# Gated cross-attention and FFN block on one core: VectorE's steps for the next tile set between the splits of the third stage, and the splits of the second stage's last tile set ahead of the gammas and the base

## What is computed

```
x = x + tanh(g_xattn) * xattn(layernorm(x), ctx)
x = x + tanh(g_ffn)  * ffn(layernorm(x))

xattn(x): z = self_attn(x)            # causal, Q,K,V = x@Wq1, x@Wk1, x@Wv1
          x = layer_norm(x + z) * ln1_g + ln1_b
          z = cross_attn(x, ctx)      # 77 keys
          x = layer_norm(x + z) * ln2_g + ln2_b
          z = relu(x @ fc1_w + fc1_b) @ fc2_w + fc2_b
          return layer_norm(x + z) * ln3_g + ln3_b

ffn(x):   h = layernorm(x) * ln_gamma + ln_beta
          y = silu(h @ w1 + fc1_bias)     # w1: 512 x 2048, from codes and scales
          return x + 0.5 * (y @ w2 + fc2_bias)   # w2: 2048 x 512
```

## Time and profile before

| | us |
|---|---|
| median of 3 runs | 1725.01 |
| lowest and highest | 1722.39, 1727.16 |
| the profiled execution | 1726.05 |
| its span in the trace | 1724.2 |
| TensorE busy | 1658.7 |
| VectorE busy | 836.8 |
| ScalarE busy | 570.2 |
| GpSimd busy | 362.4 |

### The profile page before, as it was taken

The page is one execution under the profiler, slowest core; times in us unless marked ns, Lnnn a source line. Parts: engine busy times, 40 slices in busy tenths (PEclk is TensorE's granted clock), DMA queues, the critical chain, the costliest instruction groups (busy, mean ns, idle before and its releaser), DMA issues.

```text
span 1724.2 us, 20645 instructions
## 1 busy us (share of the span) xinstructions
PE 1658.7 (96%) x7734; PEld 1351.6 (78%) x7734; DVE 836.8 (49%) x1720; ACT 570.2 (33%) x990; POOL 362.4 (21%) x562
## 2 busy tenths in 40 slices
PE   6999999999999998899999799999999999999999
PEld 4877888877788887678777587878787878878787
DVE  4666554477664444578888854323322232232311
ACT  4442212135222211467566433222322232232222
POOL 0121110022110101278888711000000000000000
PEclk8999999999999999699999899999999999999999
DMA  6211111131121102635545232101010101010000
GB/s 203 73 50 67 63 37 37 38 110 59 64 74 37 43 19 95 222 123 166 159 161 176 100 122 73 50 1 49 0 49 1 49 0 49 1 43 7 17 9 25
DMA packets 68824, 117.24 MB, mean 68 GB/s; under 512 B 11201, under 2 KB 13249, under 8 KB 68571
## 3 DMA queue, kind: packets, MB, share of 16 engines
q1 hardware_dynamic: 64968, 110.12, 19.6%
q10 hardware_dynamic: 3757, 5.80, 1.1%
HBM read 81.05 MB, written 34.84 MB: 67 GB/s over the span
## 4 chain that ended last, share of the span: by engine, by line
PE 86%; DVE 6%; ACT 2%; POOL 2%; DMA 2%; issue 1%; ACTq 0%; SPq 0%; DVEq 0%
PE banks L652 80%; PE banks L662 3%; PE banks L785 2%; DVE split_q L1521 1%; ACT split_q L1017 1%; DVE plain L2029 1%; DVE split L1994 1%; DVE plain L2072 1%; DVE split L1521 1%; DMA plain<-in_L_xattn_Wq 1%; DMA plain<-in_L_xattn_fc_w 1%; DMA plain<-in_x 0%; ACT split L1017 0%; POOL split L1414 0%; POOL plain L1426 0%
## 5 line engine op out<-in xcount | busy, mean ns | idle before, releaser
L652 PE MATMUL banks<-split_q,split 128*128 128x512 f32 x2328 | 572.7, 395 | 5.4 <-POOL split L1414 5.1
L652 PE MATMUL banks<-split 128*128 128x512 f32 (+4 forms) x2292 | 550.1, 390 | 20.2 <-DVE split L1521 7.6
L652 PEld LDWEIGHTS banks<-split 128*128 128x128 f32 (+3 forms) x2292 | 416.6, 187 | 123.3 <-issue 13.8
L652 PEld LDWEIGHTS banks<-split_q,split 128*128 128x128 f32 x2328 | 431.9, 189 | 97.4 <-POOL split L1414 6.5
L652 PE MATMUL banks<-split,split_q 128*128 128x512 f32 (+2 forms) x1728 | 395.7, 381 | 5.7 <-DVE split L1521 3.5
L652 PEld LDWEIGHTS banks<-split,split_q 128*128 128x128 f32 x1728 | 306.7, 190 | 62.1 <-DVE split_q L1521 3.3
L1521 DVE TENSOR_TENSOR split<-banks,split 128x512 fp32r<-128x512 f32 (+5 forms) x232 | 146.9, 639 | 176.6 <-ACT split L1017 175.9
L1994 DVE TENSOR_TENSOR split<-plain,split 128x512 fp32r<-128x512 f32 x128 | 88.3, 690 | 258.0 <-ACT split L1318 258.0
L1017 ACT ACTIVATE split<-banks 128x512 fp32r<-128x512 f32 (+5 forms) x232 | 124.7, 557 | 268.1 <-PE banks L785 207.6
L1312 ACT ACTIVATE plain<-banks,small 128x512 f32<-128x512 f32 x128 | 87.7, 685 | 285.2 <-PE banks L652 285.2
L1521 DVE TENSOR_TENSOR split_q<-banks,split_q 128x512 fp32r<-128x512 f32 x68 | 46.8, 688 | 245.7 <-ACT split_q L1017 245.6
(11 more groups left out here) (155 smaller groups left out, 1263.5 us busy)
## 6 DMA issues: line engine op xcount, KB each, us to landing
plain<-in_x SPq DMA_DIRECT2D x64, 256.0 KB, 2.8
xo_scratch<-plain SPq DMA_DIRECT2D x32, 256.0 KB, 2.0
x_scratch<-plain SPq DMA_DIRECT2D x32, 256.0 KB, 2.0
plain<-x_scratch SPq DMA_DIRECT2D x32, 256.0 KB, 2.9
tile_x<-xo_scratch SPq DMA_DIRECT2D x32, 256.0 KB, 3.1
xg_scratch<-tile_x SPq DMA_DIRECT2D x32, 256.0 KB, 2.0
out<-plain SPq DMA_DIRECT2D x32, 256.0 KB, 2.1
tile_x<-x_scratch SPq DMA_DIRECT2D x28, 256.0 KB, 4.6
```

The costliest lines, as they stand in the source:

```text
L652: mm = nc.tensor.matmul(out, left(c, l), right(c, r), start=start and c == 0 and (l, r) == PASSES[0], stop=stop and c == chunks - 1 and (l ...
```

## The change

It has no new instruction and takes none away; the order changes in three streams.

VectorE, third stage: in the unit of block k's transposes the bias addition to base goes away and comes in the unit behind it, after that unit's lo_hid3 and h_shift; and h_scale of block k + 1 goes in front of lo_h.

GpSimd, second stage, last tile: lo_hid 0 and 1 are set ahead of gain_x2 of block 2, lo_hid 2 and 3 ahead of that of block 3, and root_y of tile 6, block 3, goes between lo_hid 0 and 1.

ScalarE, second stage, last tile: the wait for tile 6 and base_x of block 0 go behind relu and hi_hid of hidden part 3.

```diff
@@ ScalarE, step2
                 hi_hid(t, 2)
                 if ahead:
                     hi_unit(2 * t)
-                else:
-                    act.wait_ge(xg_ready, t * BT)
-                    base_x(0, 0, 0, x1b[:, 0])
                 relu(t, 3)
                 hi_hid(t, 3)
                 if not ahead:
+                    act.wait_ge(xg_ready, t * BT)
+                    base_x(0, 0, 0, x1b[:, 0])
                     nc.scalar.preload_act_table(ACT.Silu)
@@ GpSimd, step2
             def step2(t):
-                if t:
+                if t + 1 == NT:
+                    lo_hid(t, 0)
                     root_y(t - 1, 3)
-                gain_x2(t, 2)
-                lo_hid(t, 0)
-                gain_x2(t, 3)
-                lo_hid(t, 1)
-                if t + 1 == NT:
+                    lo_hid(t, 1)
+                    gain_x2(t, 2)
                     lo_hid(t, 2)
                     lo_hid(t, 3)
+                    gain_x2(t, 3)
                     lo_w(2 * t + 2)
...
+                if t:
+                    root_y(t - 1, 3)
+                gain_x2(t, 2)
+                lo_hid(t, 0)
+                gain_x2(t, 3)
+                lo_hid(t, 1)
                 lo_hid(t, 2)
@@ VectorE, tile3
                     if not last:
-                        if f in TURN_AT:
-                            k = TURN_AT.index(f)
-                            x = base[:, 1 - slot, k]
-                            lo_h(t + 1, 1 - slot, k)
-                            dve.wait_ge(base_made, (t + 1) * BT + k + 1)
-                            nc.vector.tensor_tensor(x, x, bias3, ALU.add).then_inc(bias_added, 1)
-                        if f == TURN_AT[0] - 3:
-                            stats_x3(p3, base[:, 1 - slot], (b_in[1 - slot], (t + 1) // 2 * 16 + 16 * (1 - slot)))
                         if f + 2 in TURN_AT:
                             k = TURN_AT.index(f + 2)
...
                         if f + 1 in TURN_AT:
                             h_shift(t + 1, TURN_AT.index(f + 1))
+                        if f - 1 in TURN_AT:
+                            k = TURN_AT.index(f - 1)
+                            x = base[:, 1 - slot, k]
+                            dve.wait_ge(base_made, (t + 1) * BT + k + 1)
+                            nc.vector.tensor_tensor(x, x, bias3, ALU.add).then_inc(bias_added, 1)
+                        if f == TURN_AT[0] - 3:
+                            stats_x3(p3, base[:, 1 - slot], (b_in[1 - slot], (t + 1) // 2 * 16 + 16 * (1 - slot)))
+                        if f in TURN_AT:
+                            lo_h(t + 1, 1 - slot, TURN_AT.index(f))
```

## The result

| | before | after |
|---|---|---|
| median (runs) | 1722.57 us (5) | 1708.66 us (5) |
| lowest and highest | 1721.32, 1727.16 | 1707.78, 1712.23 |
| profiled execution | 1726.05 | 1708.66 |
| its span | 1724.2 | 1706.9 |

The ratio is 0.9917, with a 95% interval of 0.9901 to 0.9933. The change gains 13.9 us; 12.7 were forecast. Of the 3.6 us, 1.2 are the gain and 2.4 the level of the kernel before, whose median is 1722.57 us here and was taken as 1725.0 for the forecast.

A forecast was written before the change was run, and what follows sets the result against it. TensorE was taken to bound the kernel (86% of the span), so gains lie only where it waits. Third stage 12.0 plus second stage 0.7 made 12.7 us: 1725.0 - 12.7 = 1712.3 us, range for 8 in 10 1709.0 to 1716.0.

The forecast's parts named there:

- The third stage: VectorE's two steps moved from between lo_h and lo_hid3: 0.57 us per stall, 3 per tile, 7 tiles, 12.0 us gained.
- the upper bound of 12.7: Third stage: weight loads' 21.9 us wait less 9.2 us kept by ScalarE's copy leaves at most 12.7 us to gain.
- ScalarE's copy next late: Third stage: lo_hid3 then waits for ScalarE's copy of the hidden values, so 0.33 us per first weight load stays.
- The chain to the third transposes: Second stage's last tile: relu 3 and its copy leave the chain over VectorE and ScalarE, bringing transposes 1.35 us earlier.
- the sum by that rule alone, 11.3 us: Whole kernel: GpSimd's contention lengthens both h_scales, second stage loses 0.7 us, so 12.0 - 0.7 = 11.3 us gained.
- Half of the 1.35 us lost to the clock: End of second stage: TensorE at 1.2 GHz keeps only 0.7 us of the 1.35 us.
- A: End of second stage: TensorE gets the full 4.2 us by which mlp_out(7,0) ends earlier; 1708.8 us; chance 0.11.
- B: End of second stage: longer low-clock stretch and lengthened h_scales lose 2.7 us; 1715.7 us; chance 0.14.
- C: Third stage: ScalarE's copy comes later than read, only part of the stalls goes, 6.0 us gained; 1718.3 us; chance 0.03.
- D: Third stage: late base_x delays the moved bias add and later splits, slower; 1743 us at 4.5 us late; chance 0.02.
- E: Third stage: VectorE's order doesn't set the stalls, no change; 1725 us; chance 0.02.

The follow-up runs named there:

- pool_only: Kernel before with only GpSimd's new order in the second stage's last tile; third transposes 21.83 us behind the tile's first product, end of stage 41.66 us.
- late_copy: Changed kernel with ScalarE's copy and VectorE's split of the third stage's transposes one unit later; 1704.54 us, ratio 0.9884 to the kernel before.
- third_only: Kernel before with only VectorE's new order in the third stage; ratio 0.9918 to the kernel before.
- second_only: Kernel before with only GpSimd's and ScalarE's new orders in the second stage's last tile; ratio 0.9993 to the kernel before.
- after_again: The changed kernel measured once more, nothing else altered; 1709.70 us, ratio 0.9913 to the kernel before.
- turn_later: Changed kernel with TensorE taking mlp_out(7,1) ahead of the third transposes in the second stage's last tile; ratio 0.9919 to the kernel before.
- gain_last: Changed kernel with GpSimd's gain_x2 of block 3 behind the weight split in the second stage's last tile; third transposes 21.49 us, end of stage 42.55 us.
- best: late_copy plus gain_last's step of GpSimd's gain_x2 behind the weight split; 1706.68 us, ratio 0.9892 to the kernel before.

## Why the prediction came out as it did

**The third stage: right in cause, low by 1.7 us.** It was 13.7 us, not 12.0, and above the upper bound of 12.7. The step that failed is the size of one stall, 6.72 less 6.15 us, taken from one pair of places. Both numbers lie at the end of a spread that makes the difference small. From transposes to the end of the second layer the 21 stalled places of before take 6.72 to 6.77 us, and its seven places with k = 3 6.13 to 6.15; after the change all 28 take 6.09 to 6.15, most of them 6.10 or 6.11. So the prediction took the shortest stall and the longest place without one. The distances say the same: a mean of 12.20 us over the 21 of before and of 11.56 over those of after, 0.64 us each in place of 0.57, or 13.5. The bias add in front of lo_hid3 doesn't explain the longer k = 3, since pool_only still has it there and takes 6.10 to 6.11; why these places spread by 0.05 us stays open. The upper bound took time in the weight loads' row for time on the path. That row fell by 13.1 us (21.9 to 8.8) where the path gained 13.7, and by 8.8 in late_copy where it gained 5.3, so it bounds nothing.

**ScalarE's copy next late: right.** The remaining wait is 28 x 0.31 us, and late_copy removed it. That the bias and h_scale are covered in their new places was right too; base_x shows no wait for h_scale after.

**The chain to the third transposes: right, 1.30 us measured and 1.35 forecast.** mlp_out(7,0) ended early without any effect, as said. The account inside was less right. One h_scale pair took 2.37 us in place of 1.42 as foreseen, and the two h_shifts 2.44 in place of 3.48:

```profile
961.78 2.37 DVE L2033 SCALAR_TENSOR_TENSOR plain<-tile_x,small,plain 128x512 f32<-128x512 f32 x2 [1.32 <-issue]
964.07 2.44 DVE L2038 SCALAR_TENSOR_TENSOR plain<-plain,small 128x512 f32<-128x512 f32 x2
```

The Trainium skill's rule (GPSIMD Engine Reference, Specifications) holds by these rows: a VectorE step with two SBUF inputs is longer where GpSimd works beside it, 1.64 against 0.75 us for shift_y. But the sum by that rule alone, 11.3 us, was further off than the rows' sum.

**Half of the 1.35 us lost to the clock: wrong in its outcome.** The end of the second stage came 1.26 us earlier, not 0.7. The loss itself came about as foreseen: TensorE ran at the level of 1.2 GHz behind the third transposes, and mlp_out(7,1) took 5.01 us to the next transposes (977.20 to 982.21) in place of 4.49 (980.87 to 985.36), 0.52 more; at the level of 2.4 GHz 12 matmuls take 2.72. The step that failed is that the prediction followed the path only as far as the third transposes. It left out the next wait in the same stretch, that for lo_hid3(0,0). Before, TensorE stood there; from the start of the 48 matmuls to unit 2's first layer it took 14.19 us (985.72 to 999.91), and after 13.71 (982.57 to 996.28). These 0.48 us gave nearly all of the 0.52 back.

So in the kernel before TensorE's speed behind the transposes doesn't matter: in third_only the same product took 4.07 us, TensorE stood 0.80 us at the end instead of 0.19, and the stretch was 42.60 us in both. What sets the end there is VectorE's chain to lo_hid3(0,0). In the profiled execution after, lo_hid3(0,0) comes 1.48 us earlier (38.97 to 37.49) and TensorE shows no idle time in front of its product, so that its own work, at the low clock too, sets the end. second_only is the same case with mlp_out(7,1) at 4.81 us in place of 5.18, and its stretch is 41.00 in place of 41.34. But it isn't so in each execution of the changed kernel: in after_again that product took 4.47 us, TensorE stood 0.40 us for lo_hid3(0,0), and the stretch was 41.29.

Here are TensorE's rows of third_only for it:

```profile
978.84 4.07 PE L652 MATMUL banks<-split_q,split 128*128 128x512 f32 x12
...
995.07 2.98 PE L652 MATMUL banks<-split 128*128 128x512 f32 x12 [0.80 <-issue]
```

**Rivals.** A (4.2 us at the end of the second stage) is out: TensorE was ready 4.39 us early and gained nothing by it. That the measured median, 1708.66, lies at A's 1708.8 is chance. B's longer low stretch didn't come; the granted clock of 975 to 984 was 0.62, not 0.50:

```profile
975.00:984.00 9.00, 7.57 (x26) 6.26 (x27) 6.24 (x14) 4.35 (x8) 4.23 (x4) 0.62 0.28 76
```

Over 970 to 990 us, which holds the whole low stretch in each trace, the granted clock is 0.74 before, 0.83 after and 0.83 in third_only. So the stretch was shorter and not longer, and not because of the new order, since third_only has the old one there.

The Trainium skill's sentence that the throttled state is the default and activity releases it (TensorE: Matmul & The Clock Gate, What's actually happening) fits the rows of turn_later above, where the level fell after an idle time of 2.65 us. It gave no support to B's sign: the longer idle piece of after (4.39 us) was followed by a shorter low stretch than before. C, D and E did not happen.

**The level of the time.** The gain of 12.7 was subtracted from 1725.0, the median of three runs. With five it was 1722.57, and the changed kernel was measured in the same runs. In the later comparisons the kernel before had medians of 1724.75 (15 runs), 1724.55 (9) and 1724.13 (7), with single runs from 1721.6 to 1727.7. The profiled executions show where this comes from: the last tile of the second stage starts between 952.96 and 958.31 us, over the same code. The 13 traces place most of it. The second stage's first transposes start between 688.35 (turn_later) and 692.19 us (gain_last). From there to the transposes that stand 212 to 214 us ahead of the last tile's first product it is 50.8 to 55.5 us, and only 1.3 us of difference arise behind them. In that entry into the second stage the low clock differs: over 680 to 745 us the granted clock is 0.74 in best and 0.76 before, which have 55.5 and 53.1 us there, and 0.82 in after and turn_later, which have 52.2 and 51.6. That the clock is the reason is not shown. By the traces the miss of 3.6 us is 1.7 of the third stage and 0.6 of the second; the 1.3 left over, found by subtraction, is of the level. By the medians alone it is 1.2 of the gain and 2.4 of the level. The range allowed for 1 us of level. With 1722.57 in place of 1725.0 the same gain of 12.7 us would have given 1709.9.

## What to carry over

Count a stall from events in one trace that repeat (here 21 distances between turn units) rather than from one pair, and forecast the ratio with its own spread before the absolute time. When steps are taken out from in front of a critical one, ask for the next latest input: here the first of two steps gave 0.62 us and the second almost nothing, and the next gain lay on ScalarE's order, not on VectorE's. An idle time on TensorE isn't worth its length if another engine's chain ends at a later wait: filling most of 4.39 us brought the product behind that later wait forward by 0.18 us and made a gap in front of it, behind which the clock fell and cost 1.65 us. And a path must be followed through every wait up to the stage's end: the clock's 0.52 us were lost and given back at the next one.

## What the runs showed of the hardware that was not expected

A wait in the weight loads' row is not time on the path one for one: in late_copy 0.31 us less there were 0.19 us of time per turn unit, and in the change itself 13.1 us less went with 13.7 us of time. VectorE's step of 0.75 us with two SBUF inputs took 1.64 beside GpSimd's, so that moving GpSimd's work alone (pool_only) shortened VectorE's chain by 0.96 us, of which 0.90 is the length of that one step. And TensorE's level of 1.2 GHz at the end of the second stage had no effect on the stretch's length while VectorE's chain bounded it (12 matmuls in 4.07 and 4.66 us, 42.60 us in both), but it had where TensorE did not wait at the end (4.81 and 5.18 us, 41.00 and 41.34 us).
